# Attention and FP8 feed-forward kernel: chunk 0 with x in four loads, keys projected first, and Wq turned between the projections

## What is computed

```python
q, k, v = xn @ Wq.T, xn @ Wk.T, xn @ Wv.T        # xn = layernorm(x); 32 query heads, 8 key/value heads, 16 wide
scores = einsum('bsqhd,bthd->bqhst', qh, kh) * scale
a_dot = einsum('bqhst,bthd->bsqhd', softmax(scores), vh)
a_mem = elu(q) @ memory / (elu(q) @ memory_norm)
x = x + a_dot * (1 - w) + a_mem * w               # w = sigmoid(memory_weight)
x = x + fp8_roundtrip(layernorm(x)) @ (weight * weight_scale).T
```

## Time and profile before

| | |
|---|---|
| Time, median of 3 runs | 2101.21 us (2100.49 to 2101.35) |
| The profiled execution: time | 2100.72 us |
| Its span, first to last instruction | 2099.0 us |
| PE, ACT, DVE, POOL busy | 97%, 93%, 55%, 4% of the span |
| First projection starts, first scores start | 16.23 us, 233.57 us into the span |

### The profile page before, as it was taken

One profiled execution on the slowest core, in us unless ns is written; L12 is line 12 of the kernel. 1 busy time (PEld: TensorE's weight loads), 2 busy tenths in 40 slices (PEclk: granted clock), 3 DMA queues, 4 the chain that ended last, 5 costly groups with the idle time before them and its releaser, 6 DMA issues.

```text
span 2099.0 us, 63902 instructions
## 1 busy us (share of the span) xinstructions
PE 2045.4 (97%) x27826; PEld 883.7 (42%) x27826; DVE 1148.8 (55%) x1768; ACT 1942.9 (93%) x2180; POOL 83.6 (4%) x135
## 2 busy tenths in 40 slices
PE   7999799999999999999999999999999999999996
PEld 4555343344444444444343444444434444444442
DVE  5666554445555545555455555455554455554556
ACT  4444699999999999999999999999999999999995
POOL 3222000000000000000000000000000000000000
PEclk9999999999999999999999999999999999999998
DMA  5554411111111211121111211111112111121111
GB/s 188 177 176 137 123 47 47 47 42 33 47 48 47 67 30 40 47 67 47 47 33 42 67 47 47 41 51 45 48 47 67 35 40 47 47 67 47 30 40 41
DMA packets 119739, 127.96 MB, mean 61 GB/s; under 512 B 13696, under 2 KB 96000, under 8 KB 119488
## 3 DMA queue, kind: packets, MB, share of 16 engines
q1 hardware_dynamic: 117424, 121.42, 20.4%
q10 hardware_dynamic: 2064, 2.69, 0.4%
HBM read 86.57 MB, written 37.49 MB: 59 GB/s over the span
## 4 chain that ended last, share of the span: by engine, by line
PE 92%; DVE 3%; SPq 2%; ACT 1%; issue 1%; DMA 0%; ACTq 0%; POOL 0%; DVEq 0%
PE ps L722 42%; PE ps L744 42%; PE ps L673 3%; PE ps L789 1%; PE ps L775 1%; PE ps L687 1%; DVE pool L887 1%; SPq L339 1%; SPq L327 1%; PE ps L649 1%; DVE parts L912 0%; DVE norm L916 0%; DVE y_out L994 0%; DMA mem_aug<-in_memory_norm 0%; PE ps L767 0%
## 5 line engine op out<-in xcount | busy, mean ns | idle before, releaser
L623 ACT ACTIVATE pool<-ps 128x1024 f32<-128x1024 f32 x1984 | 1833.9, 1133 | 17.9 <-PE ps L722 13.1
L722 PE MATMUL ps<-q_st,k_st 99*32 99x512 bf16 x16384 | 1105.2, 379 | 10.0 <-DMA v_st<-v_aug 9.9
L744 PE MATMUL ps<-pool,v_st 128*32 128x512 f32 (+1 forms) x8704 | 1077.1, 567 | 0.3 <-ACT pool L623 0.3
L722 PEld LDWEIGHTS ps<-q_st,k_st 99*32 99x32 bf16 x16384 | 445.0, 96 | 801.9 <-issue 412.4
L744 PEld LDWEIGHTS ps<-pool,v_st 128*32 128x32 f32 x8704 | 276.4, 111 | 211.5 <-ACT pool L623 1.2
L1076 DVE SCALAR_TENSOR_TENSOR parts<-parts 128x1024 f32<-128x1024 f32 x192 | 235.2, 1225 | 6.6
L1083 DVE STREAM_TRANSPOSE by_token<-ps 128x512 f32<-128x512 f32 x64 | 45.9, 717 | 290.6 <-PE ps L744 290.6
L1062 DVE TENSOR_SCALAR parts<-ps 128x512 f32<-128x512 f32 x128 | 88.6, 692 | 132.4 <-PE ps L722 132.4
L1138 DVE SCALAR_TENSOR_TENSOR y_out<-ps,scalars,resid 128x512 f32 x28 | 21.0, 751 | 216.4 <-PE ps L775 216.4
L673 PE MATMUL ps<-pool,wqT 128*128 128x512 f32 x256 | 113.9, 592 | 0.0
L578 ACT ACTIVATE parts<-ps 128x512 bf16<-128x512 f32 x40 | 23.9, 597 | 75.7 <-PE ps L673 75.7
(11 more groups left out here) (123 smaller groups left out, 823.2 us busy)
## 6 DMA issues: line engine op xcount, KB each, us to landing
q_st<-q_aug SPq DMA_DIRECT2D x384, 64.0 KB
v_st<-v_aug SPq DMA_DIRECT2D x64, 256.0 KB
q_aug<-parts SPq DMA_DIRECT2D x96, 128.0 KB
k_st<-k_aug SPq DMA_DIRECT2D x64, 192.0 KB
sigma_kept<-y_out SPq DMA_DIRECT2D x32, 256.0 KB, 3.2
k_st<-k_aug SPq DMA_DIRECT2D x64, 128.0 KB
wqT<-sigma_kept SPq DMA_DIRECT2D x32, 256.0 KB, 3.2
resid<-in_x SPq DMA_DIRECT2D x7, 1024.0 KB, 8.0
```

The costliest lines, as they stand in the source:

```text
L623: act.activation(held[:, half_u * 2 * CH:half_u * 2 * CH + 2 * CH], sc[unit % SLOTS].rearrange("p a b -> p (a b)"), ACT.Exp, scale=EXP_UNIT)\
L722: last = pe.matmul(dst[VW * c:VW * c + VW, :], k_st[0:AUG, par, keys:keys + VW], q_st[0:AUG, par, q * CH:q * CH + CH], start=True, stop=True)
L744: last = pe.matmul(acc[par][VW * c:VW * c + VW, :].rearrange("v (i s) -> v i s", s=VW)[:, places, :], v_st[:, par, j, :], by_place[:, c, p ...
```

## The change

It rewrites the start and renumbers the projections in all chunks.

- x of chunk 0 comes in four DMAs, one per tile, each with a semaphore, and DVE takes a tile's statistics when it has come. Wq comes in four DMAs, one per query strip. All ten of these loads stay on ACT's queue, in the order x, Wk, Wq 0 to 3, Wv; the five small loads move to SP's queue.
- In every chunk the keys are o = 0 and the query strips are o = 1 to 4.
- PE turns Wk and the first strip of Wq, then half of chunk 0's `xn`; the other half is turned in the middle of the key projection. The other three strips and Wv are turned after the projections o = 0 to 3 of chunk 0, in one PSUM bank, and ACT copies each of them right behind `first_part`.
- ACT makes `e_neg` after the copies of chunk 0's turned `xn`.
- POOL's memset of `k_st` comes after the first `rstd_of`.

```diff
+        w_tp = [vp, n2] + [vp] * QG
...
-            sp.wait_ge(wkv_loaded, 32)
+            sp.sem_inc(x_loaded[0], 16)
+
+            sp.dma_start(mem_w, memory_weight.partition_broadcast(P)).then_inc(small_loaded, 16)
+            sp.dma_start(ws_col, weight_scale.partition_broadcast(P)).then_inc(small_loaded, 16)
+            sp.dma_start(s_raw[:, :], input_scale.partition_broadcast(P)).then_inc(small_loaded, 16)
+            sp.dma_start(mem_aug[:, 0:KV], memory).then_inc(small_loaded, 16)
+            sp.dma_start(mem_aug[:, KV:KV + 1], memory_norm).then_inc(small_loaded, 16)
+            sp.wait_ge(w_loaded[QG + 1], 16)
...
-                        if o < QG:
-                            sp.wait_ge(sigma_ready, (c + par) * QG + o + 1)
-                            sp.dma_start(sigma_kept[bass.ds((c + par) * QG + o, 1), :, :].rearrange("a p s -> (a p) s"),
-                                         sigma[:, o, :]).then_inc(sigma_stored[o], 16)
+                        q = o - 1
+                        if o != KEYS:
+                            sp.wait_ge(sigma_ready, (c + par) * QG + q + 1)
+                            sp.dma_start(sigma_kept[bass.ds((c + par) * QG + q, 1), :, :].rearrange("a p s -> (a p) s"),
+                                         sigma[:, q, :]).then_inc(sigma_stored[q], 16)
...
-            pool_e.wait_ge(ones_set, 2)
-            pool_e.memset(k_st[ROWS:P, :, :], 1.0).then_inc(ones_set, 1)
             pool_e.wait_ge(consts_set, 6)
-            pool_e.wait_ge(ones_set, 3)
 
...
             rstd_of(0, 0)
             pool_e.wait_ge(rstd_ready, 1)
+            pool_e.memset(k_st[ROWS:P, :, :], 1.0).then_inc(ones_set, 1)
+            pool_e.wait_ge(ones_set, 3)
...
-            act.dma_start(resid[:, 0:TPC, :], x_tiles[:, 0:TPC, :]).then_inc(x_loaded[0], 16)
-            act.dma_start(wq_raw[:, :, :], Wq.rearrange("(a p) i -> p a i", p=P)).then_inc(wq_loaded, 16)
-            act.dma_start(wkv_raw[:, 0, :], Wk).then_inc(wkv_loaded, 16)
-            act.dma_start(wkv_raw[:, 1, :], Wv).then_inc(wkv_loaded, 16)
-            act.dma_start(mem_w, memory_weight.partition_broadcast(P)).then_inc(small_loaded, 16)
-            act.dma_start(ws_col, weight_scale.partition_broadcast(P)).then_inc(small_loaded, 16)
-            act.dma_start(s_raw[:, :], input_scale.partition_broadcast(P)).then_inc(small_loaded, 16)
-            act.dma_start(mem_aug[:, 0:KV], memory).then_inc(small_loaded, 16)
-            act.dma_start(mem_aug[:, KV:KV + 1], memory_norm).then_inc(small_loaded, 16)
+            for t in range(TPC):
+                act.dma_start(resid[:, t, :], x_tiles[:, t, :]).then_inc(x_first[t], 16)
+            act.dma_start(wkv_raw[:, 0, :], Wk).then_inc(w_loaded[0], 16)
+            for q in range(QG):
+                act.dma_start(wq_raw[:, q, :], Wq[q * P:q * P + P, :]).then_inc(w_loaded[1 + q], 16)
+            act.dma_start(wkv_raw[:, 1, :], Wv).then_inc(w_loaded[QG + 1], 16)
...
-            act.wait_ge(small_loaded, 80)
-            act.activation(e_neg, mem_w, ACT.Exp, scale=-1.0).then_inc(e_neg_ready, 1)
-
-            for j in range(KT + 2):
...
+            def copy_weight(b):
+                act.wait_ge(w_turned, b + 1)
+                dst = wkT[:, :, :] if b == 0 else wvT[:, :, :] if b == QG + 1 else wqT[:, :, (b - 1) * P:b * P]
+                act.activation(dst, w_tp[b].rearrange("p (k o) -> p k o", k=KT), ACT.Copy,
+                               scale=SCALE / EXP_UNIT if b == 0 else 1.0).then_inc(w_copied, 1)
...
                     first_part(c, o)
-                    if o < QG:
+                    if c == 0 and o + 2 < QG + 2:
+                        copy_weight(o + 2)
+                    if o != KEYS:
...
+            for b in range(2):
+                copy_weight(b)
             copy_xnT(0, 0, range(KT), first=True)
+            act.wait_ge(small_loaded, 80)
+            act.activation(e_neg, mem_w, ACT.Exp, scale=-1.0).then_inc(e_neg_ready, 1)
...
+            pe.wait_ge(consts_set, 1)
+
+            def turn_weight(b):
+                pe.wait_ge(w_loaded[b], 16)
+                pe.wait_ge(w_copied, max(b - 1, 0) if b < 3 else b)
...
+                    last = pe.transpose(w_tp[b][:, k * P:k * P + P], src, ident[:, :])
                 last.then_inc(w_turned, 1)
+
...
+                    if c == 0:
+                        pe.wait_ge(w_copied, o + 1)
                     for k in range(KT):
+                        if c == 0 and o == 0 and k == KT // 2:
+                            turn_xn(0, range(KT // 2, KT))
                         if o == 0:
                             pe.wait_ge(xnT_ready, c * KT + k + 1 + TWO_FREE)
-                        w = wqT[:, k, o * P:o * P + P] if o < QG else wkT[:, k, :]
+                        w = wkT[:, k, :] if o == KEYS else wqT[:, k, (o - 1) * P:o * P]
                         last = pe.matmul(pj[i % len(pj)], w, xnT[:, par, k, :], start=(k == 0), stop=(k == KT - 1))
                     last.then_inc(proj_ready, 1)
+                    if c == 0 and o + 2 < QG + 2:
+                        turn_weight(o + 2)
...
-            pe.wait_ge(w_copied, 2)
-            turn_xn(0, range(KT))
-            pe.wait_ge(w_copied, KT + 2)
-            pe.wait_ge(scal, 4)
+            for b in range(2):
+                turn_weight(b)
+            turn_xn(0, range(KT // 2))
+            pe.wait_ge(consts_set, 6)
...
-            dve.wait_ge(x_loaded[0], 16)
-            statistics(0)
+            for t in range(TPC):
+                dve.wait_ge(x_first[t], 16)
+                last = dve.bn_stats(stats[:, t, :], resid[:, t, :])
+            last.then_inc(stats_ready, 1)
             dve.wait_ge(stats_ready, 1)
             mean_and_variance(0)
             normalise(0, 0)
...
-                    if o < QG:
-                        dve.wait_ge(epos_ready, c * QG + o + 1)
-                        dve.wait_ge(sigma_stored[o], 16 * (c + 1))
-                        dve.scalar_tensor_tensor(sigma[:, o, :], epos[:, o % 2, :], -1.0, here, ALU.add, ALU.max)\
+                    q = o - 1
+                    if o != KEYS:
+                        dve.wait_ge(epos_ready, c * QG + q + 1)
...
-                    if o == QG:
+                    if o == KEYS:
                         dve.tensor_reduce(k_sum[:, c:c + 1], here, AX.X, ALU.add)
                     dve.tensor_tensor(here, here, parts[:, o, 0, :], ALU.subtract).then_inc(rest_ready, 1)
```

More of the change, by code:

```diff
@@ L28 @@
 VW = 32
+KEYS = 0
 SPLIT = 3
@@ L201, in attention_ffn @@
         x_loaded = [sem(f"x_loaded{i}") for i in range(2)]
-        wq_loaded = sem("wq_loaded")
-        wkv_loaded = sem("wkv_loaded")
+        x_first = [sem(f"x_first{t}") for t in range(TPC)]
+        w_loaded = [sem(f"w_loaded{b}") for b in range(QG + 2)]
         small_loaded = sem("small_loaded")
@@ L322, in store_parts @@
                             rows = slice(i * DH, i * DH + DH)
-                            if o < QG:
-                                dst = q_aug[bass.ds((c + par) * HEADS, HEADS), rows, o * CH:o * CH + CH]
+                            if o != KEYS:
+                                dst = q_aug[bass.ds((c + par) * HEADS, HEADS), rows, q * CH:q * CH + CH]
                             else:
@@ L580, in exp_neg @@
             def exp_neg(c, o):
-                i = c * QG + o
-                act.activation(neg[:, o % 2, :], pj[(c * (QG + 1) + o) % len(pj)], ACT.Relu, scale=-1.0).then_inc(neg_ready, 1)
+                q = o - 1
+                i = c * QG + q
+                act.activation(neg[:, q % 2, :], pj[(c * (QG + 1) + o) % len(pj)], ACT.Relu, scale=-1.0).then_inc(neg_ready, 1)
                 if i >= 2:
@@ L585, in exp_neg @@
                 act.wait_ge(neg_ready, i + 1)
-                act.activation(epos[:, o % 2, :], neg[:, o % 2, :], ACT.Exp, scale=-1.0).then_inc(epos_ready, 1)
+                act.activation(epos[:, q % 2, :], neg[:, q % 2, :], ACT.Exp, scale=-1.0).then_inc(epos_ready, 1)
             def second_part(c, o):
@@ L634, in _ @@
             pe.sem_inc(v_proj_ready, ONE_FREE)
-            pe.wait_ge(consts_set, 6)
-            pe.wait_ge(wq_loaded, 16)
-            for j in range(KT + 2):
-                if j == KT:
-                    pe.wait_ge(wkv_loaded, 32)
-                for a in range(KT):
-                    src = wq_raw[:, a, j * P:j * P + P] if j < KT else wkv_raw[:, j - KT, a * P:a * P + P]
-                    last = pe.transpose(ps[:, j, a * P:a * P + P], src, ident[:, :])
+            pe.wait_ge(consts_set, 1)
+            def turn_weight(b):
+                pe.wait_ge(w_loaded[b], 16)
+                pe.wait_ge(w_copied, max(b - 1, 0) if b < 3 else b)
+                for k in range(KT):
+                    if b == 0:
+                        src = wkv_raw[:, 0, k * P:k * P + P]
+                    elif b == QG + 1:
+                        src = wkv_raw[:, 1, k * P:k * P + P]
+                    else:
```

(8 more changed lines are left out.)

13 lines of the change are left out of this document (5 added, 8 removed).

## The result

| | before | after |
|---|---|---|
| Time, median of 7 runs | 2100.49 us (2099.99 to 2101.61) | 2107.70 us (2106.41 to 2109.07) |
| The profiled execution: time, span | 2100.72, 2099.0 us | 2107.60, 2105.9 us |
| Chunk 1's first projection | 42.10 us | 47.79 us |
| Chunk 7's first projection | 198.24 us | 203.74 us |
| First scores | 233.57 us | 238.77 us |

The changed kernel is slower by 7.2 us: 1.0034 times the time before, interval 1.0023 to 1.0044. The forecast was 2105.0, and 2107.7 lies above its range. The likeliest case of the prediction was no change to speak of; what came is its case "slower", which had a chance of 0.39. The kernel before stood at 2100.49 here and at 2101.20 to 2101.59 beside the experiments; experiment 12, the changed kernel measured again, finds 6.0 us instead of 7.2.

What follows compares the result with a forecast made beforehand. It took PE in the attention stage, untouched by the change, as the bound (PE busy 97%). Start and chunk 0 3.15, small loads 0.2 and hand-over 0.5 gave +3.85 us: median 2105.0 us, range 2101.3 to 2107.0.

Steps and rivals of the forecast that it cites:

- likeliest case: Whole kernel: +3.85 us, just under the 4.2 us that can be told from no change; chance 0.42.
- case "slower": Whole kernel: slower by more than 4.2 us, through a later clock rise on PE; chance 0.39.
- the memset: Beside chunk 0's normalise: holds DVE for its whole length, so xn is ready at 14.0 us instead of 12.5.
- the walk: Chunk 0 followed engine by engine: chunk 1's first projection starts 3.15 us later, near 45.4 instead of 42.10.
- Small loads on SP's queue: At the start: 0.4 us of DMA time, half ahead of x's last tile, +0.2 us; bounds 0 and 1.6.
- x in four tiles: At the start: the fourth tile lands when x did, 6.18 us; aggregation starts at 6.85 instead of 8.68.
- The first rival: Chunk 0: the memset doesn't hold DVE, xn comes at 10.6 us, sum +0.4, time 2101.6 us; chance 0.17.
- PE's clock: Chunk 0: half speed until 3.95 us after xn at 14.0, so full speed from 17.9 us.
- The second rival: Chunk 0: PE's idle 5.4 us delays its clock rise; +4.9 us, 2106.1, if at 20.8 or later; chance 0.39.
- The period stays: Undisturbed chunks with keys first: DVE's shifted work causes no new wait, so the period stays 25.87 us.
- SP at the hand-over: Hand-over to attention: one more store ahead of the first elu's load, for which PE waits, +0.5 us.

Runs made afterwards that it cites:

- experiment 12: The changed kernel itself, unaltered, profiled and measured once more; 2107.58 us, 1.0030 times the kernel before.
- kernel 2: The changed kernel with the five small loads back on ACT's queue, behind Wv; 2106.05 us, 1.0025 times the kernel before.
- kernel 3: The changed kernel with the memset waiting for xn and the five small loads back on ACT's queue; 2102.67 us, 1.0010 times the kernel before.
- kernel 1: The changed kernel with the memset of k_st waiting until xn of chunk 0 is ready; 2104.46 us, 1.0015 times the kernel before.
- kernel 9: The kernel before with only the five small loads moved to the front of SP's queue; 2102.35 us, 1.0005 times the kernel before.
- kernels 6: kernel 3 with 28 and then 16 identity transposes keeping PE busy before xn; 2101.34 us, 1.0000 times the kernel before.
- kernel 7: kernel 3 with ACT copying a turned strip of Wq after Exp, not before ReLU; 2102.16 us, 1.0004 times the kernel before.
- kernel 4: The kernel before with only the memset of k_st moved behind the first rstd_of; 2103.75 us, 1.0012 times the kernel before.
- kernel 5: The kernel before with only the projections renumbered, keys first; 2102.13 us, 1.0005 times the kernel before.
- kernel 8: The kernel before with V and the first elu loaded earlier in SP's queue at the hand-over; 2100.71 us, 0.9997 times the kernel before.

## Why the prediction was wrong

It had the memset, the largest term, and most of the walk, and fell 2.7 us short (3.0 by the two profiled executions, 2104.6 against 2107.60). Its sum of +3.85 us stood just under the 4.2 that it took for the smallest visible change, so its favourite was no change, and that was missed too.

- **Step "Small loads on SP's queue": +0.2 forecast, 1.3 measured in the traces and 1.6 to 1.8 in the time. This is the step that failed.** It treated the DMA engines as a shared belt: 0.4 us of their time for the small loads, half of it ahead of x. With these loads back on ACT's queue x's last tile was used 1.35 us earlier (kernel 2 against the changed kernel, 7.04 and 8.39) or 1.31 (kernel 3 against kernel 1, 6.88 and 8.19), and the medians fell by 1.65 and 1.79. That is near the bound of 1.6 that I gave, the whole stretch that the small loads took in the kernel before, and far from their busy share of it. What the windows show is not a belt that is full: 80 and 97 GB/s at a share of 0.41 and 0.35, the engines mostly idle. The Trainium skill, "DMA: Bandwidth & Descriptors", section "Queues, rings and completion order", says that each DMA engine takes turns between the queues that have work for it, packet by packet. By that, small loads on a second queue are served among the big ones and not behind them. It doesn't explain why x, under way beside them in kernel 9, was not late (6.12), nor engines that idle, and that cause stays open.
- **"x in four tiles": "it should land when x did, 6.18": up to 0.9 too early.** The other part of x's delay of 2.2 us is here. With the small loads away the last tile was used at 7.04 and 6.88 (kernels 2 and 3), and at 6.00 and 5.95 in kernels 6 and 7, which have the same loads and ran on another chip. The argument that the same bytes lie ahead left out that four DMAs are issued over 1.83 us, so that the last two no longer stand ahead of another queue's traffic; what makes the landing differ where there is no such traffic was not tested.
- **The memset: right.** One `tensor_scalar` of 3.81 us, which ended 0.27 us after the memset (10.98 + 3.81 = 14.79 against 11.01 + 3.51 = 14.52; I had taken 0.28 from the earlier trace rows), and then the others at their usual pitch. It held the first instruction, although the trace has that one begin 0.03 us earlier. I forecast 3.4 us more for `normalise` and it is 3.25 (5.17 - 1.92). Kernels 1 and 3 give it 3.2 and 3.4 us of the time. With the rule that I cited from "SBUF — State Buffer" of the Trainium skill the trace agrees, also for a memset that only writes: the two exclude one another. The first rival, a harmless memset, is excluded.
- **PE's clock: right in size.** The first eight turns of `xn` took 1.97 us and the later eight 1.04, so full speed came after 18.2 and before 20.9; from the spacing of the records it is 20.2, 4.05 us after `xn`, where I had 3.95. (The granted clock of the profile reads 1.00 in all of this stretch. That it was half is read from the rows: in kernel 4 eight turns take the same 1.97 us where the granted clock reads 0.50.) The second rival, a late rise, did not occur there: what passed 4.2 us was mostly its other half, the small loads. A late rise did occur at the hand-over, where the granted clock was at half until 245.5, 6.7 us after the first scores began; before the change it was 4.2 us after:

```profile
244.00:245.00 1.00, 1.00 (x12) 0.21 (x7) 0.00 (x0) 0.55 (x1) 0.00 (x0) 0.50 0.58 180
245.00:246.00 1.00, 1.00 (x20) 0.45 (x16) 0.00 (x0) 0.24 (x1) 0.00 (x0) 0.76 0.40 126
```

  It cost nothing here, because PE still waited 0.79 us for the first elu after it.
- **The walk through chunk 0: right as a sum.** From `xn` to chunk 1 I had 31.25 us, measured 31.63. Inside it two errors partly cancel: the key projection took 0.6 longer than forecast (24.25 - 16.16 = 8.1 against 7.5), and from there to chunk 1 it was 0.2 shorter (23.54 against 23.75), where by kernel 7 only one of the two copies counts. So chunk 1 at +5.69 instead of +3.35 is 1.96 for x beyond the 0.2, and 0.38 for this.
- **"The period stays": right**, 25.87 from chunk 1 to 5, and chunk 6 0.19 shorter.
- **"SP at the hand-over", +0.5: 1.58 measured, the second term that was short.** PE waits for the elu's load as forecast (0.79 us), and the queue has the one store more. But from its first issue to that load SP takes 48.22 us (201.94 to 250.16) instead of 46.69 (196.44 to 243.13): 0.5 is the store, and 1.0 lies in issues that take longer. Keys first alone, kernel 5, lengthens the queue too, but there PE came late for another reason. From chunk 7's first projection to the memory product both profiles of the changed kernel take 1.5 us longer than before (49.23 and 49.18 against 47.65); kernels 1, 2, 3, 5, 6 and 7, also with keys first, take 0.4 to 1.3 longer, and kernel 4, in the old order, 0.6. Before and after the change, single issues on SP's queue take 1.0 to 1.6 us instead of 0.61. After it there are more of them: nine over 0.7 us instead of six. One is in this part of the chain of the kernel after:

```profile
235.10 0.61 SPq L338
235.75 0.61 SPq L338
...
238.22 1.16 SPq L338
```

  How much of that falls into the backlog differs from kernel to kernel, by more than the store costs. Why the changed kernel has most in both of its profiles stays open: that is 1.1 us of the sum.

By these terms: 3.85 (forecast) + 1.96 (x: 1.1 for the small loads beyond their 0.2, the rest for the split) + 0.38 (the walk) + 1.08 (hand-over) - 0.37 (chunk 6 and the attention stage) = 6.90, the difference of the spans. The failed step and the split of x account for most of what is missing; the hand-over's part is measured, and its cause is not.

## What to carry to other kernels

A load that is moved to an idle queue to get it out of the way can hold up the big loads that are still to come: look at the GB/s of the first microseconds, and not at how few bytes it moves or how small its busy share is, and issue what is needed first as one DMA ahead of everything small. GpSimd work that has nothing to do with the critical path belongs beside DVE's idle time or behind DVE's critical instructions, never at the semaphore that releases them. And a lead gained at the start is worth what the next hand-over lets through: read there which wait comes second, and third, before paying for the lead.

## What the runs showed of the hardware

- Five small loads (three of them broadcasts to 128 partitions) on a second queue took the transfers down to 80 and 97 GB/s in two windows of 1 us, at a DMA share of 0.41 and 0.35; with the same loads on the first queue, behind the big ones, these windows have 264 and 344 GB/s (kernel 3). x's last tile was used 1.3 us later, and Wq in kernel 9 1.9 us later, though issued 0.3 us ahead of the first small load. The load ahead of Wq, issued 0.8 us ahead of the small ones, was not delayed (6.12).
- A GpSimd memset of 3.51 us held a DVE `tensor_scalar` that had begun 0.03 us before it for 3.81 us; undisturbed it is 0.53. Four executions of three kernels show it (the changed kernel twice, 2 and 4).
- GpSimd's reduction over partitions has a row of 0.37 us, but came 5.8 us after its engine's last row. With no load left to wait for, PE started 2.2 us after the flag's last instruction (231.11 + 0.15 to 233.49, kernel 8).
